# Expert rounds of a mixture-of-experts layer: the scatter of the last expert's rows ahead of the next gather

## The chip, the cores and the metric

The kernel runs on one core of one Trainium2 chip. The metric is the time of one execution on the device in microseconds (us); the figure for a kernel is the median of its runs.

## What is computed

The input is 8192 tokens of 512 float32 values. The reference is one transformer layer: layernorm, attention, layernorm and residual, then layernorm, a mixture of experts, layernorm and residual. Cut to the part that matters here:

```python
scores = softmax(xf @ gate_w.T)                 # 64 experts, 6 chosen per token
buf_tok = ...                                   # (E=64, CAP=128): rows of each expert, T where empty
gx = xp[buf_tok]                                # gather: 128 rows for each expert
g, u = split(einsum('ech,ehi->eci', gx, gate_up_proj), 2)
eo = einsum('eci,eih->ech', silu(g) * u, down_proj) * buf_w[..., None]
routed = zeros.at[buf_tok].add(eo)              # scatter with addition
shared = silu(xf @ Ws_gate) * (xf @ Ws_up) @ Ws_down
```

An expert takes at most 128 tokens. `gate_up_proj` is 512x384 for each expert and `down_proj` 192x512, all in float32.

## The kernel before, in words

Three stages follow one another. `token_pipeline` does attention, the two norms, the gate and the shared expert, 128 tokens at a time, and leaves three arrays in DRAM: `xf_d` (the normed tokens with their gate weights, 576 values a row), `acc_d` (the shared expert's output, on which the experts add) and `x1_d` (the residual). `experts` runs the 64 experts. `last_norm` reads `acc_d` back, norms it and adds the residual. The change is in `experts` alone.

In `experts` five engines run the same pipeline of iterations `j`, from -4 to 64, each with its own program order; semaphores tie them together. What belongs to expert e is spread over several iterations:

- **DVE** (the block from L1086): `gidx(j+2)` (L1088) copies the 128 row numbers of expert j+2 to one of two buffers that the gather reads. It waits for the rows of expert j, whose gather used the same buffer, and for the indices. `sidx(j-1)` (L1092) copies the row numbers of expert j-1 for the scatter, after waiting for the scatter of expert j-3 to have landed (`added`). Then `gate(j)` (L1096, which waits for the rows of j), the two halves of the gated product (L1099 and L1104, after ScalarE's tanh), the finding of the indices of expert j+3 (L1110 to L1119) and the mask `sel` for expert j+4 (L1122, L1127).
- **Pool** (from L1134) issues both indirect DMAs. The gather of expert j+2 (L1141, 128 rows of 2304 bytes) waits for `gidx(j+2)`, for `e_xT(j)` and for `gate(j)`: the last two free the one of two buffers `xg` that it fills. The scatter with addition of expert j-1 (L1148, 128 rows of 2048 bytes) waits for the output rows `eo(j-1)`, for `sidx(j-1)`, and for the scatter of j-2 to have landed, since two experts can add to the same row.
- **PE**: in iteration j, in this order: the gate and up product `gu(j)` (L1008), the transpose of the hidden rows of j-1 (L1015), the two small products that find the rows of expert j+3 (L1022, L1023), the transpose `xT(j+1)` of the gathered rows of j+1 (L1029, waits for the gather of j+1), and the down product `out(j-1)` (L1037).
- **ACT**: the copy of the transposed hidden rows of j-1 (L1050), the copy of the transposed gathered rows of j+1 (L1054), the copy `eo(j-1)` of the output from PSUM (L1058, waits for `out(j-1)` and for the scatter of j-3), tanh of j (L1062).
- **SP**: once `out(e)` is done, it loads the weights of expert e+4 into the place of e's, 768 KB and 384 KB (L133, L134), and in the rounds of the first loop, after every second expert, also 512 KB of the residual (L975). Four experts' weights are in SBUF at a time.

Pool, like the other engines, issues its instructions strictly in the order written, and a wait holds all that is behind it. In the order of the kernel before, Pool's sequence is: gather(j+2), scatter(j-1), gather(j+3), scatter(j), and so on. So the gather that follows the scatter of expert e is that of expert e+4.

Of the kernel before, what the change touches and what calls it, by code (L numbers as in the profile page):

```python
# [34 lines left out]
U32 = mybir.dt.uint32  # L35
# [65 lines left out]
def settle(eng):  # L101

    eng.nop(nofuse=True)  # L103
# [782 lines left out]
def experts(nc, cst, w1, w2, w_in, load_expert, xf_d, acc_d, rank_d, x1_d, res, res_in):  # L886


    with ExitStack() as ctx:
        def sb(name, shape, dt=F32):  # L890
            return ctx.enter_context(nc.sbuf_tensor(name, shape, dt))

        def count(name, per=1, n=1, place=0):
            return Count(ctx.enter_context(nc.semaphore(name)), per, E, n, place)
# [18 lines left out]
        idx = sb("idx", [CAP, E], I32)  # L913
        gidx = sb("gidx", [CAP, 2, 1], I32)
        sidx = sb("sidx", [CAP, 2, 1], I32)
        xg = sb("xg", [P, 2, D + E])
# [10 lines left out]
        x_got = [count(f"x_got{n}", 16, 2, n) for n in range(2)]  # L927
        added = count("added", 16)
        e_xT = count("e_xT")
# [7 lines left out]
        ed_gidx = count("ed_gidx")  # L937
        ed_sidx = count("ed_sidx")
        ed_gate = count("ed_gate")
# [15 lines left out]
        def active(e):  # L955
            return not isinstance(e, int) or 0 <= e < E

        def pipeline(eng, iteration):
            for j in range(FIRST, LOOP):
                iteration(j, j % NW)  # L960
            with eng.Fori(0, ROUNDS) as r:
                for u in range(NW):
                    iteration(r * NW + (LOOP + u), (LOOP + u) % NW)
            for j in range(REST, LAST):
                iteration(j, j % NW)
# [100 lines left out]
        @block.vector  # L1066
        def _(dve):
            dve.wait_ge(start, 32)
            nc.vector.tensor_copy(tri[:], c[0:NT, C_TRI:C_TRI + NT]).then_inc(setup, 1)
            nc.vector.tensor_copy(base[:, :, 0], c[0:NT, C_TILE:C_TILE + 1].broadcast_to([NT, E]))  # L1070
            nc.vector.memset(base[:, :, 2], 1.0)
            dve.wait_ge(setup, 2)
            nc.vector.tensor_copy(end[:], ends_ps[0:NT, 0:E]).then_inc(setup, 1)
            nc.vector.tensor_tensor(first[:], ends_ps[0:NT, 0:E], rank[:, :, P - 1], ALU.subtract).then_inc(setup, 1)
            dve.wait_ge(setup, 4)
            nc.vector.tensor_copy(base[:, :, 1], first[:]).then_inc(setup, 1)
            dve.wait_ge(setup, 5)

            def column(ap, e):
                return ap[:, e:e + 1] if isinstance(e, int) else ap[:, bass.ds(e, 1)]  # L1080

            def iteration(j, place):
                par = place % 2
                if active(j + 2):
                    dve.wait_ge(x_got[par].sem, x_got[par].at(j))
                    dve.wait_ge(ed_idx.sem, ed_idx.at(j + 2))  # L1086
                    settle(dve)
                    nc.vector.tensor_copy(gidx[:, par, :], column(idx[:], j + 2)).then_inc(ed_gidx.sem, 1)  # L1088
                if active(j - 1):
                    dve.wait_ge(added.sem, added.at(j - 3))  # L1090
                    settle(dve)
                    nc.vector.tensor_copy(sidx[:, 1 - par, :], column(idx[:], j - 1)).then_inc(ed_sidx.sem, 1)  # L1092
                if active(j):
                    dve.wait_ge(x_got[par].sem, x_got[par].at(j))
                    dve.wait_ge(ed_h.sem, ed_h.at(j - 1))
                    nc.vector.tensor_scalar(gate[:, par:par + 1], column(xg[:, par, D:D + E], j), 0.5, None,  # L1096
                                            ALU.mult).then_inc(ed_gate.sem, 1)
                    dve.wait_ge(ea_tanh.sem, ea_tanh.at(j))
                    nc.vector.scalar_tensor_tensor(tanh[:, par, :], tanh[:, par, :], 1.0, gu_ps[par][:, 0:I],  # L1099
                                                   ALU.add, ALU.mult).then_inc(ed_h.sem, 1)  # L1100
                    dve.wait_ge(ed_h.sem, ed_h.at(j, 1))
                    dve.wait_ge(ed_gate.sem, ed_gate.at(j))
                    dve.wait_ge(e_hT.sem, e_hT.at(j - 2))
                    nc.vector.scalar_tensor_tensor(hid[:, par, :], tanh[:, par, :], gate[:, par:par + 1],  # L1104
                                                   gu_ps[par][:, I:], ALU.mult, ALU.mult).then_inc(ed_h.sem, 1)
                if active(j + 3):
                    at = find_ps[1 - par]
                    dve.wait_ge(e_find.sem, e_find.at(j + 3))
                    settle(dve)
                    nc.vector.tensor_tensor(left[:], c[:, C_ROW:C_ROW + 1], at[:, P + 1:P + 2],  # L1110
                                            ALU.subtract).then_inc(ed_idx.sem, 1)
                    nc.vector.tensor_scalar(miss[:], at[:, P + 2:P + 3], -1.0, c[:, C_MISS:C_MISS + 1], ALU.add,
                                            ALU.mult).then_inc(ed_idx.sem, 1)
                    dve.wait_ge(ed_idx.sem, ed_idx.at(j + 3, 1))
                    nc.vector.tensor_scalar(ahead[:], at[:, 0:P], left[:, 0:1], None, ALU.is_le).then_inc(ed_idx.sem, 1)
                    dve.wait_ge(ed_idx.sem, ed_idx.at(j + 3, 3))
                    nc.vector.tensor_reduce(tin[:], ahead[:], AX.X, ALU.add).then_inc(ed_idx.sem, 1)
                    dve.wait_ge(ed_idx.sem, ed_idx.at(j + 3, 4))
                    nc.vector.scalar_tensor_tensor(column(idx[:], j + 3), at[:, P:P + 1], tin[:, 0:1], miss[:], ALU.add,  # L1119
                                                   ALU.add).then_inc(ed_idx.sem, 1)  # L1120
                if active(j + 4):
                    nc.vector.tensor_scalar(past[:], c[0:NT, C_IOTA:C_IOTA + CAP], column(first[:], j + 4), None,  # L1122
                                            ALU.is_ge).then_inc(ed_sel.sem, 1)
                    dve.wait_ge(ed_sel.sem, ed_sel.at(j + 4, 1))
                    dve.wait_ge(e_find.sem, e_find.at(j + 3))
                    settle(dve)
                    nc.vector.scalar_tensor_tensor(sel[:], c[0:NT, C_IOTA:C_IOTA + CAP], column(end[:], j + 4), past[:],  # L1127
                                                   ALU.is_lt, ALU.mult).then_inc(ed_sel.sem, 1)

            pipeline(dve, iteration)  # L1130

        @block.gpsimd
        def _(pool):
            def iteration(j, place):  # L1134
                par = place % 2
                if active(j + 2):
                    pool.wait_ge(ed_gidx.sem, ed_gidx.at(j + 2))
                    pool.wait_ge(e_xT.sem, e_xT.at(j))
                    pool.wait_ge(ed_gate.sem, ed_gate.at(j))
                    settle(pool)  # L1140
                    nc.gpsimd.indirect_dma_start(xg[:, par, :], None, xf_d, bass.IndirectOffsetOnAxis(  # L1141
                        gidx[:, par, :].bitcast(U32), 0)).then_inc(x_got[par].sem, 16)
                if active(j - 1):
                    pool.wait_ge(ea_out.sem, ea_out.at(j - 1))
                    pool.wait_ge(ed_sidx.sem, ed_sidx.at(j - 1))
                    pool.wait_ge(added.sem, added.at(j - 2))
                    settle(pool)
                    nc.gpsimd.indirect_dma_start(acc_d, bass.IndirectOffsetOnAxis(  # L1148
                        sidx[:, 1 - par, :].bitcast(U32), 0), eo[:, 1 - par, :], None,
                        compute_op=ALU.add).then_inc(added.sem, 16)  # L1150

            pipeline(pool, iteration)
            pool.wait_ge(added.sem, added.at(E - 1))
# [168 lines left out]
```

## Time and profile before

| what | value |
|---|---|
| median of 3 runs | 2307.55 us (2302.56 to 2309.64) |
| the profiled execution | 2310.43 us |
| its span | 2308.6 us |
| busy share of the span | PE 87%, DVE 62%, ACT 43%, Pool 22% |
| mean granted TensorE clock | 0.937 |
| expert rounds | from about 1675 to 2190 us |
| last_norm | from about 2190 us to the end |

The profile is of one execution, and its times run from the start of the span. The profiled execution took 1.8 us more than its span, and 2.9 us more than the median of the runs. Engine names in the rows: PE is TensorE's matmuls, PEld its weight loads, SPq the DMA queue of SyncE, POOL is GpSimd. L1148 is line 1148 of the kernel. In a timeline a row says when an instruction or a merged run of them starts, how long it lasts, and, in brackets, how long its engine was idle before and what ended that.

### The profile page before, as it was taken

Reading aid. Unit: us, or ns where it says so; the run is one execution under the profiler, and the core shown is the slowest. Engines: PE = TensorE matmul, PEld = TensorE weight load, DVE = VectorE, ACT = ScalarE, POOL = GpSimd, SP = SyncE. Lnnn points to the kernel's source line nnn. Section 1 sums busy time; section 2 is a strip of 40 time slices with the busy share of each in tenths; the row PEclk is TensorE's granted clock in tenths of the full one; section 3 lists DMA queues with packets and bytes.
Section 4 is the critical chain, followed back from the end, with each engine's and each line's share of the span. In section 5 each row is a group of like instructions: output and inputs, shape, how many; then the busy total and the mean of one; then the engine's idle time right before and its main releaser. Section 6 shows DMA issues by size and latency. Waiting matters only on the chain. (4 is left out here: it accounts for less than half of the span.)

```text
span 2308.6 us, 48488 instructions
## 1 busy us (share of the span) xinstructions
PE 2009.6 (87%) x14529; PEld 1605.4 (70%) x14529; DVE 1434.2 (62%) x3874; ACT 983.2 (43%) x1779; POOL 497.7 (22%) x741
## 2 busy tenths in 40 slices
PE   6999999999999999999999999998478777787600
PEld 4888888888888888888888888887344444444300
DVE  6677677677677677677767767766233333333298
ACT  4455555555555545545545545544112222222222
POOL 1111111111111111111111111111023333333288
PEclk8999999999999999999999999999789998898855
DMA  5333433433433333333343333332669899899597
GB/s 175 97 90 91 112 90 89 111 93 89 105 99 89 101 103 88 98 106 83 97 110 85 94 112 86 93 105 69 188 188 260 255 246 250 252 266 249 139 324 258
DMA packets 386471, 325.13 MB, mean 141 GB/s; under 512 B 286656, under 2 KB 286912, under 8 KB 386368
## 3 DMA queue, kind: packets, MB, share of 16 engines
q1 hardware_dynamic: 366912, 271.04, 41.4%
q0 software_dynamic: 14336, 35.66, 7.3%
q10 hardware_dynamic: 5184, 17.96, 2.1%
q8 instruction: 19, 0.31, 0.1%
q14 instruction: 20, 0.16, 0.0%
HBM read 203.43 MB, written 121.14 MB: 141 GB/s over the span
## 5 line engine op out<-in xcount | busy, mean ns | idle before, releaser
L864 POOL TENSOR_SCALAR ve<-mv 128x1 f32<-128x1 f32 x192 | 44.9, 234 | 1319.9 <-DVE mv L698 1319.9
L592 ACT COPY qT<-bank 48x512 f32<-48x512 f32 x256 | 268.8, 1050 | 63.9 <-PE bank L435 59.2
L459 PE MATMUL score_ps<-kT,qT 48*64 48x64 f32 x4096 | 264.9, 286 | 3.0 <-ACT kT L592 3.0
L459 PEld LDWEIGHTS score_ps<-kT,qT 48*64 48x64 f32 x4096 | 219.5, 147 | 48.7 <-issue 48.7
L715 DVE SCALAR_TENSOR_TENSOR th<-th,bank 128x192 f32<-128x192 f32 x128 | 45.3, 354 | 296.8 <-ACT th L628 296.8
L1099 DVE SCALAR_TENSOR_TENSOR tanh<-tanh,e_gu 128x192 f32<-128x192 f32 x64 | 22.7, 354 | 287.6 <-ACT tanh L1062 284.2
L1008 PE MATMUL e_gu<-w,xgT 128*128 128x384 f32 x512 | 189.1, 514 | 1.3 <-ACT xgT L1054 1.3
L442 PE MATMUL bank<-wgu,xfT 128*128 128x416 f32 x512 | 187.9, 367 | 2.4 <-ACT xfT L592 2.4
L443 PE MATMUL bank<-wgu,xfT 128*128 128x416 f32 x512 | 180.4, 352 | 0.0
L1008 PEld LDWEIGHTS e_gu<-w,xgT 128*128 128x128 f32 x512 | 105.9, 207 | 98.1 <-issue 50.4
L628 ACT ACTIVATE th<-bank 128x192 f32<-128x192 f32 x128 | 42.3, 330 | 287.4 <-PE bank L446 287.4
L1148 POOL DMA_INDIRECT acc_scratch<-eo,sidx x64 | 101.7, 1590 | 266.9 <-DMA acc_scratch<-eo,sidx 138.3
L592 ACT COPY kT<-bank 48x512 f32<-48x512 f32 x256 | 148.7, 581 | 4.7
L1037 PE MATMUL e_ps<-w,hidT 96*128 96x512 f32 x256 | 147.5, 706 | 0.9 <-ACT hidT L1050 0.9
L644 ACT ACTIVATE prob<-prob 128x512 f32<-128x512 f32 x128 | 78.8, 633 | 114.5 <-DVE prob L789 114.5
L446 PE MATMUL bank<-wgu,xfT 128*128 128x416 f32 x512 | 118.0, 353 | 0.0
L866 POOL TENSOR_TENSOR rstd<-ve,mhalf 128x1 f32<-128x1 f32 x192 | 108.8, 567 | 16.2 <-POOL ve L864 0.3
L442 PEld LDWEIGHTS bank<-wgu,xfT 128*128 128x128 f32 x512 | 97.2, 190 | 19.3 <-issue 10.6
L1054 ACT COPY xgT<-e_ps 128x512 f32<-128x512 f32 x64 | 37.4, 585 | 170.6 <-PE e_ps L1029 166.9
L442 PE MATMUL bank<-wlat,xT 128*128 128x512 f32 x256 | 108.8, 425 | 1.4 <-issue 1.4
L442 PE MATMUL bank<-wo,oT 128*128 128x512 f32 x256 | 106.8, 417 | 0.0
L443 PE MATMUL bank<-wlat,xT 128*128 128x512 f32 x256 | 102.6, 401 | 0.0
(179 smaller groups left out, 4772.2 us busy)
## 6 DMA issues: line engine op xcount, KB each, us to landing
w<-w_eg SPq DMA_DIRECT2D x64, 768.0 KB
w<-w_ed SPq DMA_DIRECT2D x64, 384.0 KB
xf_scratch<-xf SPq DMA_DIRECT2D x64, 288.0 KB, 2.1
xin<-x SPq DMA_DIRECT2D x64, 256.0 KB, 3.0
v_scratch<-v SPq DMA_DIRECT2D x64, 256.0 KB, 3.5
vbd<-v_scratch SPq DMA_DIRECT2D x128, 128.0 KB, 3.2
o_scratch<-o SPq DMA_DIRECT2D x256, 64.0 KB, 2.3
oin<-o_scratch SPq DMA_DIRECT2D x64, 256.0 KB, 2.6
```

What stands on the lines that cost most here:

```text
L442: nc.tensor.matmul(dst, a[:, 0], b[:, 0], start=(n == 0), stop=False)
L443: nc.tensor.matmul(dst, a[:, 0], b[:, 1], start=False, stop=False)
L446: last = nc.tensor.matmul(dst, a[:, 1], b[:, 0], start=False, stop=(n == len(lhs) - 1))
L459: last = nc.tensor.matmul(score_ps[64 * g:64 * g + 64, blk * 64:blk * 64 + 64], qT[:, t0:t0 + B4, :].rearrange("p t h -> p (t h)"), kT[:, ...
L592: nc.scalar.copy(dst, src).then_inc(done.sem, 1)
L644: nc.scalar.activation(pf, pf, ACT.Exp, scale=SCALE).then_inc(a_exp.sem, 1)
L715: nc.vector.scalar_tensor_tensor(th[:, n, :], th[:, n, :], 1.0, b[:, 0:I], ALU.add, ALU.mult).then_inc(d_h.sem, 1)
L864: nc.gpsimd.tensor_scalar(ve[n][:], mv[n][:, 1:2], EPS, None, ALU.add).then_inc(g_rstd[n].sem, 1)
L866: nc.gpsimd.tensor_tensor(rstd[n][:], ve[n][:], mhalf[:], ALU.pow).then_inc(g_rstd[n].sem, 1)
L1008: last = nc.tensor.matmul(gu_ps[par], xgT[:, par, n, :], w1[:, place, n, :], start=(n == 0), stop=(n == KD - 1))
L1037: last = nc.tensor.matmul(out_ps, hidT[:, n, :], w2[0:PI, (place - 1) % NW, n, :], start=(n == 0), stop=(n == 1))
L1148: nc.gpsimd.indirect_dma_start(acc_d, bass.IndirectOffsetOnAxis(sidx[:, 1 - par, :].bitcast(U32), 0), eo[:, 1 - par, :], None, compute_op= ...
```

## The change

In every iteration Pool issues the scatter of expert j-1 first and the gather of expert j+2 second, each with the waits that it had. DVE makes the copies of their indices in that order too: `sidx(j-1)` first, then `gidx(j+2)`. Nothing is added or removed, and no buffer or wait value is changed. The gather that follows the scatter of expert e is now that of expert e+3.

```diff
             def iteration(j, place):
                 par = place % 2
+                if active(j - 1):
+                    dve.wait_ge(added.sem, added.at(j - 3))
+                    settle(dve)
+                    nc.vector.tensor_copy(sidx[:, 1 - par, :], column(idx[:], j - 1)).then_inc(ed_sidx.sem, 1)
                 if active(j + 2):
                     dve.wait_ge(x_got[par].sem, x_got[par].at(j))
                     dve.wait_ge(ed_idx.sem, ed_idx.at(j + 2))
                     settle(dve)
                     nc.vector.tensor_copy(gidx[:, par, :], column(idx[:], j + 2)).then_inc(ed_gidx.sem, 1)
-                if active(j - 1):
-                    dve.wait_ge(added.sem, added.at(j - 3))
-                    settle(dve)
-                    nc.vector.tensor_copy(sidx[:, 1 - par, :], column(idx[:], j - 1)).then_inc(ed_sidx.sem, 1)
...
             def iteration(j, place):
                 par = place % 2
-                if active(j + 2):
-                    pool.wait_ge(ed_gidx.sem, ed_gidx.at(j + 2))
-                    pool.wait_ge(e_xT.sem, e_xT.at(j))
-                    pool.wait_ge(ed_gate.sem, ed_gate.at(j))
-                    settle(pool)
-                    nc.gpsimd.indirect_dma_start(xg[:, par, :], None, xf_d, bass.IndirectOffsetOnAxis(
-                        gidx[:, par, :].bitcast(U32), 0)).then_inc(x_got[par].sem, 16)
                 if active(j - 1):
                     pool.wait_ge(ea_out.sem, ea_out.at(j - 1))
                     pool.wait_ge(ed_sidx.sem, ed_sidx.at(j - 1))
                     pool.wait_ge(added.sem, added.at(j - 2))
                     settle(pool)
                     nc.gpsimd.indirect_dma_start(acc_d, bass.IndirectOffsetOnAxis(
                         sidx[:, 1 - par, :].bitcast(U32), 0), eo[:, 1 - par, :], None,
                         compute_op=ALU.add).then_inc(added.sem, 16)
+                if active(j + 2):
+                    pool.wait_ge(ed_gidx.sem, ed_gidx.at(j + 2))
+                    pool.wait_ge(e_xT.sem, e_xT.at(j))
+                    pool.wait_ge(ed_gate.sem, ed_gate.at(j))
+                    settle(pool)
+                    nc.gpsimd.indirect_dma_start(xg[:, par, :], None, xf_d, bass.IndirectOffsetOnAxis(
+                        gidx[:, par, :].bitcast(U32), 0)).then_inc(x_got[par].sem, 16)
```

## Rows read from the trace of the kernel before

**Rows 1.** The page, the span in 40 equal slices (tenths; PEclk: granted clock).
```profile
PE   6999999999999999999999999998478777787600
...
PEclk8999999999999999999999999999789998898855
DMA  5333433433433333333343333332669899899597
```

**Rows 2.** Windows view: the steady expert rounds in one stretch (PE, PEld, DVE, ACT, POOL busy).
```profile
1695.00:2173.00 478.00, 378.69 (x1218) 212.95 (x1217) 162.04 (x723) 108.05 (x244) 156.59 (x122) 0.90 0.90 249
```

**Rows 3.** Line view of L1148, 1695 to 2173 us: scatters; what ended Pool's idle time.
```profile
L1148 POOL DMA_INDIRECT acc_scratch<-eo,sidx x62: 1567/1588/1693, 1694.9 to 2172.9; - x62
...
  DMA acc_scratch<-eo,sidx: 134.1, 35
  ACT eo L1058: 71.2, 16
  DVE gate L1096: 42.1, 8
  DVE gidx L1088: 8.6, 2
```

**Rows 4.** Lines view, 1695 to 2173 us: PE's transposes of gathered rows.
```profile
L1029 PE MATMUL e_ps<-e_c,xg 128*128 128x128 f32 x244 | 49.5, 332 | 45.1 <-DMA xg<-xf_scratch,gidx 42.9
```

**Rows 5.** Timeline: from a late gather to the next scatter, clock at its lower level.
```profile
1890.11 0.17 PE L1023 MATMUL e_find<-base,sel 64*128 x1
1890.99 0.15 DVE L1092 COPY sidx<-idx 128x1 int32 x1 [1.08 <-DMA acc_scratch<-eo,sidx]
...
1894.21 1.13 PE L1029 MATMUL e_ps<-e_c,xg 128*128 128x128 f32 x4 [3.93 <-DMA xg<-xf_scratch,gidx]
...
1895.13 3.62 PE L1037 MATMUL e_ps<-w,hidT 96*128 96x512 f32 x4
...
1898.87 0.58 ACT L1058 COPY eo<-e_ps 128x512 f32<-128x512 f32 x1 [2.90 <-PE e_ps L1037]
...
1900.36 1.59 POOL L1148 DMA_INDIRECT acc_scratch<-eo,sidx  x1 [5.85 <-ACT eo L1058]
...
1902.76 0.17 PE L1023 MATMUL e_find<-base,sel 64*128 x1
```

**Rows 6.** Timeline of Pool: gathers (L1141) and scatters (L1148) in turn.
```profile
1884.58 0.99 POOL L1141 DMA_INDIRECT xg<-xf_scratch,gidx  x1 [1.32 <-PE e_ps L1029]
...
1908.68 1.59 POOL L1148 DMA_INDIRECT acc_scratch<-eo,sidx  x1 [3.85 <-DMA acc_scratch<-eo,sidx]
1910.57 0.99 POOL L1141 DMA_INDIRECT xg<-xf_scratch,gidx  x1 [0.30 <-PE e_ps L1029]
1914.50 1.59 POOL L1148 DMA_INDIRECT acc_scratch<-eo,sidx  x1 [2.93 <-DMA acc_scratch<-eo,sidx]
```

**Rows 7.** Line view of L1141, all 64 gathers: from issue to landing.
```profile
DMA to landing us min/median/max: 3.5/6.5/9.6
```

**Rows 8.** Timeline of SP's queue: loads issued after a down product has ended.
```profile
1899.00 0.34 SPq L133 DMA_DIRECT2D w<-w_eg  x1
1899.54 0.33 SPq L134 DMA_DIRECT2D w<-w_ed  x1
1900.19 0.36 SPq L975 DMA_DIRECT2D res<-x_scratch  x1
1905.69 0.33 SPq L133 DMA_DIRECT2D w<-w_eg  x1
```

**Rows 9.** The same for the gathers issued at 1884.58 and at 1903.84 us.
```profile
DMA to landing us min/median/max: 9.6/9.6/9.6
...
DMA to landing us min/median/max: 4.7/4.7/4.7
```

**Rows 10.** Windows view around that late gather (columns as in rows 2, then PEclk, DMA share, GB/s).
```profile
1890.00:1894.00 4.00, 0.28 (x2) 0.15 (x2) 0.31 (x2) 0.00 (x0) 2.07 (x2) 0.98 0.74 194
1894.00:1896.00 2.00, 1.79 (x6) 1.27 (x7) 0.00 (x0) 0.58 (x1) 0.51 (x1) 0.50 0.93 150
1896.00:1899.00 3.00, 3.00 (x5) 1.34 (x4) 0.00 (x0) 0.13 (x1) 0.00 (x0) 0.50 0.27 84
...
1902.00:1904.00 2.00, 1.88 (x12) 1.19 (x11) 0.73 (x4) 0.61 (x2) 0.16 (x1) 1.00 1.00 290
```

**Rows 11.** Timeline: the next round, clock at its upper level.
```profile
1903.00 0.72 PE L1029 MATMUL e_ps<-e_c,xg 128*128 128x128 f32 x4
...
1903.56 1.88 PE L1037 MATMUL e_ps<-w,hidT 96*128 96x512 f32 x4
```

## Prediction

> **What bounds the kernel now.** I began with the page's forty slices: the expert rounds are the stretch near slices 29 to 38, where PE is no longer full and the DMA engines are [rows 1]; only that stretch is touched. The windows view puts 62 scatters, thus 61 rounds, into it: from the scatter of expert 0 at 1694.9 to that of expert 61 at 2172.9 it is 478.0 us, **7.84 us a round** [rows 2, 3]. PE works 378.69 us of it, the DMA engines are 0.90 busy, so no engine alone fills it; it is a ring of waits with little slack. Pool's idle time before a scatter ends 35 times with the landing of the scatter before, 16 times with the output copy `eo`, 8 times with `gate` and 2 with `gidx`: the last two are waits of the gather that Pool has in front of the scatter [rows 3]. The transposes of the gathered rows already wait 42.9 us in the stretch for their DMA [rows 4]. So gathers come just in time or late though each is issued as early as its buffer is free. That is the row on which the case turns.
>
> **The change, part by part.** No instruction is added or removed: 64 gathers, 64 scatters and 128 small copies stay, at the same durations. Only order moves.
>
> DVE's swap. `sidx(j-1)` now stands ahead of `gidx(j+2)`, so its wait for scatter j-3 holds back `gidx`, `gate` and all behind. In the trace `sidx` waits for that scatter now and then (1.08 us in one row, [rows 5]), but then behind `gidx`. With scatters a longer round apart, as found below, scatter j-3 has landed by then. Cost zero; the cover is the length of the round. If it is gone, the same 1.08 us would fall on `gidx`, and Pool's gather behind it.
>
> Pool's swap. Before, the gather of e+4 followed the scatter of e. Now it is the gather of e+3. But the order on PE is transpose(e+3), then down product(e+1): iteration j has xT(j+1) ahead of out(j-1). And scatter(e+1) needs that product. So there is a closed chain, one turn for each expert: scatter(e) issued, gather(e+3) issued behind it, rows landed, xT(e+3), out(e+1), copy eo(e+1), scatter(e+1). Before, the same gather was issued one scatter earlier and its landing lay beside a whole round. Each turn is now the sum of all its steps:
>
> - scatter's start to gather's start on Pool: 1910.57 - 1908.68 = 1.89 us, where the gather waited for nothing else [rows 6]. All the gather's own waits, `gidx`, `e_xT(j)` and `gate(j)`, are of earlier work and are met;
> - gather issued to landed: the trace has 3.5 at least, 6.5 in the median and 9.6 at most [rows 7]. The stretch now has its DMA engines 0.90 busy; the same bytes over a round of 13 us make them 0.90 x 7.84 / 13 = 0.54 busy, so it should be under the median. It is not the floor, since SP puts weights, and every second time the residual, into the queues just after the down product, 0.2 to 1.4 us ahead of the scatter [rows 5, 8]. A gather 3.48 us behind such a scatter took 4.7 [rows 5, 9]. I take **5.0**, halfway between 3.5 and 6.5;
> - landing to transpose: the gather issued at 1884.58 landed 9.6 us later, at 1894.18, and its transpose began at 1894.21; I take 0.1, rounded up [rows 5, 6, 9];
> - transpose to down product: 1895.13 - 1894.21 = 0.92 us, and the product 3.62 us, where PE had stood idle for 3.93 us and the granted clock was 0.50, the 1.2 GHz level [rows 5, 10]. At the upper level it is 0.56 and 1.88 [rows 11];
> - down product's end to the start of `eo`: 1898.87 - 1898.75 = 0.12; `eo`'s start to the scatter's start: 1900.36 - 1898.87 = 1.49 [rows 5].
>
> Which clock? From the down product's end at 1898.75 PE is done with its other work of the round at 1902.93 (gu, hidden transpose, find), 4.2 us later [rows 5]. The gather lands 0.12 + 1.49 + 1.89 + 5.0 = 8.5 us after that end. So PE stands idle 4.3 us in every round, longer than the 3.93 us after which [rows 5] show the slow pair. I take the lower level for transpose and down product in all rounds, and the same cover says that the gate and up product costs nothing even when slow.
>
> A turn: 1.89 + 5.0 + 0.1 + 0.92 + 3.62 + 0.12 + 1.49 = **13.14 us**. The other ring, scatter to landing to next scatter, is shorter (1914.50 - 1908.68 = 5.82 where it bound, [rows 6]) and no longer decides; the waits for it go, and the one for the gathered rows takes their place on PE. Weights are loaded three rounds ahead, so they are not late. From scatter 0 to scatter 61 there are 61 turns, as gathers 3 to 63 all stand behind a scatter. Ahead of scatter 0 and after scatter 61 nothing changes, nor in the other stages. Sum: 61 x (13.14 - 7.84) = **+323 us**. The profiled execution, 2310.43, would become 2633.7; it stands 2.9 above the median of the runs, so I forecast 2307.55 + 323 = **2631 us**.
>
> Bounds of the landing, the only term without a row in its new place: at 3.5 the turn is 11.64 and the sum +232; at 6.5 it is 14.64 and +415; at the 9.6 of the slowest gather it would be 17.74 and +604, which every round would have to reach.
>
> **Rivals.**
>
> 1. The gather lands at its floor, 3.5 us, since traffic has thinned: 61 x (11.64 - 7.84) = +232, **2540 us**. For it: 84 GB/s only in one stretch right after a late gather [rows 10]. Against it: the loads of [rows 8] are issued anew each round just ahead. The Trainium skill, DMA: Bandwidth & Descriptors, section Anatomy of one DMA, fits such a transfer as about 2.0 us plus its bytes over 436 GB/s; for 128 rows of 2304 bytes that is an estimate of 2.7 us, with which a turn would be 10.8 and the time some 2490. The shortest of the 64 gathers here took 3.5, so the trace does not reach that figure. Chance 0.13.
>
> 2. The gather lands as now, 6.5 us or somewhat more, because what it meets is not the mean traffic but the burst just issued: 61 x (14.64 - 7.84) = +415, **2722 us**. For it: the median of all gathers [rows 7], many of which, as in [rows 6], stand straight behind a scatter. Chance 0.14.
>
> 3. The clock stays at its upper level, as in rounds whose gather is in time: the turn is 13.14 - (0.92 - 0.56) - (3.62 - 1.88) = 11.04, the sum +195, **2503 us**. Against it: [rows 5, 10]. Chance 0.07.
>
> 4. The other side, faster. The scatter is no longer held by the gather's waits: 42.1 + 8.6 = 50.7 us of Pool's idle time before scatters in the stretch [rows 3]. If the chain above did not bind, all of it could come back: 2307.55 - 50.7 = **2257 us**. It decides when the gather lands within 7.84 - (0.1 + 0.56 + 1.88 + 0.12 + 1.49) = 3.7 us of the scatter's issue, which is 1.8 us after its own issue; the shortest is 3.5. Chance 0.02.
>
> 5. The change does nothing that can be measured, if Pool's order did not bind at all (a gather that is late either way). Then 2307 us. Against: the gather is issued 1.89 us behind a scatter that needs the product before it, by program order. Chance 0.01.
>
> **How the numbers follow.** The forecast has 0.63. It is the likeliest case alone, not a mean. The range of 8 in 10 holds the forecast with landings from 3.2 to 6.6, at 61 us of time for each us of landing, and with them rivals 1 and 2: **2520 to 2730**. Rival 3, the far ends and 4 and 5 are left out. A measurement of this kernel can tell about 0.3% from no change; faster has 0.02, the same 0.01, slower 0.97: even the lowest turn I can build from rows, 1.89 + 3.5 + 0.1 + 0.56 + 1.88 + 0.12 + 1.49 = 9.54 us, is above 7.84.
>
> **What the changed profile would show.** If right: the stretch of expert rounds lasts some 320 us more, and the other two stages are as before. Pool's scatters wait for the copy `eo` nearly every time and hardly ever for a landing, each gather starts about 1.9 us behind its scatter, and the transposes' wait for the gathered rows grows from 42.9 us to about 61 x 4.3 = 260 us. The mean landing is near 5.0. The four matmuls of the down product take 3.6 us in almost every round, and the granted clock is well under 0.90. DMA share in the stretch falls from 0.90 to about 0.54. If the down products stay at 1.9 us, rival 3 holds; if landing is at 3.5 or 6.5, rival 1 or 2. I would be wrong at the root if PE did not wait for gathers longer than now, or if a scatter still waited for the scatter before it.

## The result and the profile after

The changed kernel takes **2647.88 us** in the median (2643.41 to 2650.97), the kernel before 2305.49 in the same comparison: a ratio of **1.148, 95% interval 1.145 to 1.151**. The forecast was 2631, the range 2520 to 2730. The profiled execution has a span of 2648.5 us, 339.9 more than before.

One stretch grew, that from the first scatter to the 62nd. First the line view of the scatters in it (now L1141); then, from its lines view, the down product, the scatters and the transposes:

```profile
L1141 POOL DMA_INDIRECT acc_scratch<-eo,sidx x62: 1575/1588/1632, 1694.3 to 2512.9; - x62
...
  ACT eo L1058: 631.7, 60
  issue: 23.1, 2
```
```profile
L1037 PE MATMUL e_ps<-w,hidT 96*128 96x512 f32 x244 | 216.0, 1039 | 0.0
L1141 POOL DMA_INDIRECT acc_scratch<-eo,sidx x62 | 98.5, 1588 | 654.8 <-ACT eo L1058 631.7 <-issue 23.1
...
L1029 PE MATMUL e_ps<-e_c,xg 128*128 128x128 f32 x244 | 66.9, 426 | 293.4 <-DMA xg<-xf_scratch,gidx 293.4
```

818.6 us for 61 rounds is **13.42 us a round**, against 7.84 [rows 3], and 61 x 5.58 = 340 is the whole difference. Pool no longer waits for the landing of a scatter, for `gate` or for `gidx`, which were 134.1, 42.1 and 8.6 us [rows 3]: 60 of 62 times it waits for the output copy. PE's wait for the gathered rows went from 42.9 us [rows 4] to 293.4. The windows view of the stretch, with columns PE, PEld, DVE, ACT and POOL busy, granted clock, DMA share and GB/s, answers to [rows 2]:

```profile
1694.00:2513.00 819.00, 484.23 (x1219) 262.06 (x1218) 163.00 (x724) 108.04 (x244) 158.18 (x123) 0.75 0.50 146
```

The DMA engines move the same data at a share of 0.50 where it was 0.90; the granted clock is 0.75 for 0.90, and PE's busy time has risen by 105 us for the same matmuls. One pair of rounds shows the whole closed chain. Timeline, Pool:

```profile
1965.56 1.59 POOL L1141 DMA_INDIRECT acc_scratch<-eo,sidx  x1 [9.50 <-ACT eo L1058]
1967.45 1.01 POOL L1149 DMA_INDIRECT xg<-xf_scratch,gidx  x1 [0.31 <-issue]
1980.10 1.59 POOL L1141 DMA_INDIRECT acc_scratch<-eo,sidx  x1 [11.63 <-ACT eo L1058]
1981.99 1.02 POOL L1149 DMA_INDIRECT xg<-xf_scratch,gidx  x1 [0.30 <-issue]
1992.49 1.59 POOL L1141 DMA_INDIRECT acc_scratch<-eo,sidx  x1 [9.48 <-ACT eo L1058]
```

PE:

```profile
1973.94 1.13 PE L1029 MATMUL e_ps<-e_c,xg 128*128 128x128 f32 x4 [5.80 <-DMA xg<-xf_scratch,gidx]
1974.86 3.62 PE L1037 MATMUL e_ps<-w,hidT 96*128 96x512 f32 x4
...
1986.34 1.13 PE L1029 MATMUL e_ps<-e_c,xg 128*128 128x128 f32 x4 [3.66 <-DMA xg<-xf_scratch,gidx]
1987.26 3.62 PE L1037 MATMUL e_ps<-w,hidT 96*128 96x512 f32 x4
```

And the line view of L1149 for the gather issued at 1967.45, then for the one at 1981.99:

```profile
DMA to landing us min/median/max: 6.4/6.4/6.4
...
DMA to landing us min/median/max: 4.3/4.3/4.3
```

The first turn is 1980.10 - 1965.56 = 14.54 us: 1.89 from scatter to gather, 6.4 to its landing, 0.09 to the transpose, 0.92 to the down product, 3.62 of it, 1.62 to the next scatter. The second is 12.39, and all of the difference but 0.05 is the landing, 4.3. What SP issued ahead of each of the two gathers differs by one load of the residual (L975, 512 KB):

```profile
1964.31 0.34 SPq L133 DMA_DIRECT2D w<-w_eg  x1
1964.88 0.33 SPq L134 DMA_DIRECT2D w<-w_ed  x1
1965.53 0.36 SPq L975 DMA_DIRECT2D res<-x_scratch  x1
1978.72 0.33 SPq L133 DMA_DIRECT2D w<-w_eg  x1
1979.26 0.33 SPq L134 DMA_DIRECT2D w<-w_ed  x1
```

Long and short turns alternate for 56 turns, 14.65 and 12.38 us in the mean. In the last five, when SP has no more of the residual to load, all are short (12.67, 11.98, 12.78, 12.16, 12.12).

The other stages stayed: `last_norm`'s windows show the same 0.50 clock, 0.83 DMA share and 285 GB/s in both kernels.

### The profile page after: what moved, and what is told of

Read it like the earlier page. It is cut to its first block and busy times, and to the rows that moved or that the text cites. A ratio compares the mean times of both kernels' runs of the same rounds, so it can differ in the third digit from the quotient of the medians.

```text
span 2648.5 us, 48488 instructions
## 1 busy us (share of the span) xinstructions
PE 2113.9 (80%) x14529; PEld 1653.9 (62%) x14529; DVE 1434.4 (54%) x3874; ACT 983.3 (37%) x1779; POOL 498.6 (19%) x741
## 5 line engine op out<-in xcount | busy, mean ns | idle before, releaser
L1029 PE MATMUL e_ps<-e_c,xg 128*128 128x128 f32 x256 | 69.5, 422 | 295.6 <-DMA xg<-xf_scratch,gidx 295.6
L1029 PEld LDWEIGHTS e_ps<-e_c,xg 128*128 128x128 f32 x256 | 45.3, 217 | 301.4 <-DMA xg<-xf_scratch,gidx 301.3
L1141 POOL DMA_INDIRECT acc_scratch<-eo,sidx x64 | 101.6, 1587 | 663.0 <-ACT eo L1058 631.7
L1037 PE MATMUL e_ps<-w,hidT 96*128 96x512 f32 x256 | 221.8, 1019 | 0.9 <-ACT hidT L1050 0.9
L1008 PE MATMUL e_gu<-w,xgT 128*128 128x384 f32 x512 | 205.2, 549 | 1.3 <-ACT xgT L1054 1.3
L1008 PEld LDWEIGHTS e_gu<-w,xgT 128*128 128x128 f32 x512 | 120.6, 236 | 127.6 <-issue 86.2
L1037 PEld LDWEIGHTS e_ps<-w,hidT 96*128 96x128 f32 x256 | 75.5, 324 | 65.7 <-issue 64.4
L442 PE MATMUL bank<-wlat,xT 128*128 128x512 f32 x256 | 108.7, 425 | 1.4 <-issue 1.4
```

Of the source, the lines that this page charges most:

```text
L442: nc.tensor.matmul(dst, a[:, 0], b[:, 0], start=(n == 0), stop=False)
L1008: last = nc.tensor.matmul(gu_ps[par], xgT[:, par, n, :], w1[:, place, n, :], start=(n == 0), stop=(n == KD - 1))
L1029: last = nc.tensor.transpose(rowsT_ps[:, n * P:(n + 1) * P], xg[:, 1 - par, 0:D].rearrange("p (i c) -> p c i", c=KD)[:, n, :], ident)
L1037: last = nc.tensor.matmul(out_ps, hidT[:, n, :], w2[0:PI, (place - 1) % NW, n, :], start=(n == 0), stop=(n == 1))
```

## The experiments

The theory: the place of the gather behind the scatter of the expert before closes a chain, whose steps simply add up. Rivals: DVE's swap has a share; a gather behind a scatter is slow in the queue; the buffers hold the gather back; the clock is not part of it.

**The two halves of the change.** First DVE's swap alone (the first two blocks of the diff), then Pool's swap alone.

> The kernel before with DVE's swap alone; Pool keeps its order. Theory (the chain through Pool's order costs the time, DVE's swap costs nothing): 2305 us, ratio 1.00, scatter to scatter 7.8 us as before. Rival (the wait for scatter j-3 ahead of gidx and gate delays the gathers): up to 1.08 us more in each round in which sidx waits, 7 to 20 of 61, so 2315 to 2330.

> The kernel before with Pool's swap alone; DVE keeps its order. Theory: all of the loss is here, 2648 us, ratio 1.148, the same 13.4 us round as in the changed kernel. Rival (half of it is DVE's order): clearly under 2600.

Measured: DVE's swap alone 2305.13 us, ratio 1.0005 (0.9991 to 1.0018). Pool's swap alone 2647.36, ratio 1.150 (1.148 to 1.152). The whole loss is Pool's order. In DVE's half the copy `sidx` waited for a scatter 11 times, and nothing came of it:

```profile
  DMA acc_scratch<-eo,sidx: 9.5, 11
```

**Half the dose.** Pool's swap in every second iteration only (`gather()` stands for the gather with its waits).

```diff
+                if par == 0:
+                    gather()
                 if active(j - 1):
...
-                if active(j + 2):
...
+                if par == 1:
+                    gather()
```

> The changed kernel with Pool's swap in every second iteration only, the old order in the others. Theory (a closed chain scatter, gather, landing, transpose, down product, copy, scatter): every second turn is the long one of some 13.4 us, the turn between has its gathered rows already and takes about 7, so a pair takes 20.4 against 2 x 7.8: 30 x 4.7 = about +145, 2450 us, range 2420 to 2500. Rival (the gather behind the scatter just lies longer in the DMA queue): the late gathers are half as many and the loss is half, 2476, but the rounds are all alike.

Measured: 2476.27 us, ratio 1.075 (1.073 to 1.077). The total is by chance also the rival's number, so the rounds have to decide, and they are not alike. Pool's timeline (L1152 scatters, L1142 gathers):

```profile
1907.72 1.59 POOL L1152 DMA_INDIRECT acc_scratch<-eo,sidx  x1 [5.04 <-ACT eo L1058]
1909.61 1.02 POOL L1142 DMA_INDIRECT xg<-xf_scratch,gidx  x1 [0.30 <-issue]
1911.88 0.98 POOL L1142 DMA_INDIRECT xg<-xf_scratch,gidx  x1 [1.25 <-DVE gate L1096]
1921.62 1.63 POOL L1152 DMA_INDIRECT acc_scratch<-eo,sidx  x1 [8.76 <-ACT eo L1058]
1928.31 1.58 POOL L1152 DMA_INDIRECT acc_scratch<-eo,sidx  x1 [5.06 <-ACT eo L1058]
1930.20 1.04 POOL L1142 DMA_INDIRECT xg<-xf_scratch,gidx  x1 [0.30 <-issue]
1931.83 0.98 POOL L1142 DMA_INDIRECT xg<-xf_scratch,gidx  x1 [0.60 <-issue]
1942.82 1.62 POOL L1152 DMA_INDIRECT acc_scratch<-eo,sidx  x1 [10.01 <-ACT eo L1058]
```

A turn with its gather in the chain takes 13.90 and 14.51 us, the one between 6.69. The short turns are as the theory has them. The 31 long ones are 14.33 in the mean, 0.9 over the 13.4 assumed: up to the last three, the gather in the chain is here always one behind a residual load, and lands in 6.1 to 7.1 us. That is 29 us more, of which the short turns (6.69 for 7) give back 9, so it makes 20 of the 26 us by which 2450 was missed.

**The clock.** Matmuls with unused results (filler) on PE ahead of its wait for the gathered rows, first four, then seven.

```diff
+                if active(j) and active(j - 1):
+                    for n in range(4):
+                        nc.tensor.matmul(ends_ps[:, 0:C_MISS], ident, c[:, 0:C_MISS], start=True, stop=True)
                 if active(j + 1):
                     pe.wait_ge(x_got[1 - par].sem, x_got[1 - par].at(j + 1))
```

> The changed kernel with four matmuls of 390 columns (0.98 us each at the upper clock, results unused) on PE between the finding products and the wait for the gathered rows; they fill 3.9 us of the 3.6 to 5.9 us that PE stands idle. Theory (the clock's lower level after the idle wait costs 0.33 + 1.64 us of each turn): down product back to 1.9 us, round 13.4 to about 11.5, 61 x 1.97 = -120, 2528 us; 2520 to 2550 as the filler may overrun a short wait by 0.3. Rival (clock is not of the chain, or low for another reason): 2648 or more.

> As the kernel with four filling matmuls on PE, but seven. The four took 2.9 us instead of 3.9 and left the clock low in about every second round, in which the wait is the longer one (2571 us). Seven take some 5.1 us at the upper clock. Theory (clock costs 0.33 + 1.64 us of each turn, after any long idle wait): all down products at 1.9 us, but in the rounds with the short wait of 3.6 us the filler overruns it by up to 1.5 us: gain 61 x 1.97 = 120, loss up to 30 x 1.5 = 45, so 2530 to 2575 us. Rival (the level has nothing to do with the idle wait): down products of 3.6 us remain and the time is over 2600.

Measured: four give 2570.69 us (ratio 1.115, 1.113 to 1.117), outside what was expected; seven give 2561.02 (1.110, 1.107 to 1.113), inside. Two rounds of the four:

```profile
1991.42 2.89 PE L1027 MATMUL e_ps<-e_c 128*128 128x390 f32 x8
1997.12 0.75 PE L1032 MATMUL e_ps<-e_c,xg 128*128 128x128 f32 x4 [2.81 <-DMA xg<-xf_scratch,gidx]
1997.70 2.48 PE L1040 MATMUL e_ps<-w,hidT 96*128 96x512 f32 x4
...
2004.32 2.89 PE L1027 MATMUL e_ps<-e_c 128*128 128x390 f32 x8
2008.15 0.75 PE L1032 MATMUL e_ps<-e_c,xg 128*128 128x128 f32 x4 [0.95 <-DMA xg<-xf_scratch,gidx]
2008.74 1.88 PE L1040 MATMUL e_ps<-w,hidT 96*128 96x512 f32 x4
```

The filler lasts 2.89 us, not the 3.9 that I had made of eight rows of 0.49: these overlap. Where 2.81 us of idle wait are left, the down product is partly slow; where 0.95 are left, it is not. Seven of them:

```profile
1927.31 4.85 PE L1027 MATMUL e_ps<-e_c 128*128 128x390 f32 x14
1932.00 0.63 PE L1032 MATMUL e_ps<-e_c,xg 128*128 128x128 f32 x4
1932.47 1.88 PE L1040 MATMUL e_ps<-w,hidT 96*128 96x512 f32 x4
...
1938.63 4.85 PE L1027 MATMUL e_ps<-e_c 128*128 128x390 f32 x14
1944.25 0.75 PE L1032 MATMUL e_ps<-e_c,xg 128*128 128x128 f32 x4 [0.77 <-DMA xg<-xf_scratch,gidx]
1944.83 1.88 PE L1040 MATMUL e_ps<-w,hidT 96*128 96x512 f32 x4
```

The median matmul of the down product goes back from 1057 to 592 ns, and the whole product takes 1.88 us in all but three of the 61 turns. The kernel is 87 us shorter, though PE does 4.85 us more work in each round. So the clock is part of the loss: 87 of 342 us are shown, a quarter. The working from the steps, 61 x (0.33 + 1.64) = 120 us, would make it a third. What is missing fits the filler, which overruns the wait in every second round (no idle ahead of 1932.00): those turns go from 12.38 to 11.23, by 1.15 and not by 1.97, and the long ones from 14.65 to 12.63. The Trainium skill, TensorE: Matmul & The Clock Gate, Part 1, has it that the slow state is the default and activity lifts it; these runs agree, 1.88 against 3.62 us for the same four matmuls, by whether PE worked or stood in the wait ahead.

**What the slow landings meet.** The residual loads out of the rounds.

```diff
-            with sp.Fori(1, 1 + WITH_X1) as r:
-                load_round(r, True)
-            with sp.Fori(1 + WITH_X1, E // NW) as r:
+            with sp.Fori(1, E // NW) as r:
                 load_round(r, False)
+            for g in range(EARLY, NT // G):
+                load_group(g)
```

> The changed kernel with the 28 residual loads of 512 KB taken out of the rounds and issued after the last weights. Theory (the gathers of odd experts land in 6.6 us and those of even ones in 4.4 because after every second down product 512 KB more stand in the queues): all gathers land in about 4.5, scatter to scatter 12.4 in every round, 61 x 1.1 = -65 us in the rounds; the 14.7 MB come behind, 52 us at 280 GB/s, of which some 40 lie beside the last four rounds: 2590 us, 2575 to 2640. Rival (odd and even gathers differ for another reason, as the buffer or the rows): they stay at 6.6 and 4.4 and the rounds at 14.5 and 12.4.

Measured: 2611.81 us, ratio 1.132 (1.129 to 1.135). Line view of the gathers, 1700 to 2360 us, in this kernel:

```profile
L1149 POOL DMA_INDIRECT xg<-xf_scratch,gidx x52: 988/999/1019, 1709.8 to 2350.2; - x52
...
DMA to landing us min/median/max: 4.2/4.6/5.7
```

In the changed kernel the same stretch has 4.2/4.7/7.2. The landings over 5.7 us are gone, and Pool's timeline has nearly equal turns, here 12.47 and 12.67:

```profile
1909.02 1.59 POOL L1141 DMA_INDIRECT acc_scratch<-eo,sidx  x1 [9.69 <-ACT eo L1058]
...
1921.49 1.59 POOL L1141 DMA_INDIRECT acc_scratch<-eo,sidx  x1 [9.57 <-ACT eo L1058]
...
1934.16 1.59 POOL L1141 DMA_INDIRECT acc_scratch<-eo,sidx  x1 [9.77 <-ACT eo L1058]
```

The expected 2590 was missed by 22 us, though the range held. The first 59 turns are 12.59 us in the mean and not 12.4, which makes 11 of them. Nor did the loads lie beside the last four rounds: SP waits for expert 59's down product first, and its queue has them, all 28 in one run, only when two turns of the chain are left. Those two take 16.75 and 15.54 us, 7 more than two others; the rest is not traced:

```profile
2437.51 31.42 SPq L975 DMA_DIRECT2D res<-x_scratch  x28
```

**Depth, order or buffers.** Four buffers for gathered rows and their indices in three kernels; to make room, `tanh` has one buffer instead of two in all three, and two masks share one. First with the order and the depth of the changed one, and waits of two experts earlier:

```diff
-                    pool.wait_ge(e_xT.sem, e_xT.at(j))
-                    pool.wait_ge(ed_gate.sem, ed_gate.at(j))
+                    pool.wait_ge(e_xT.sem, e_xT.at(j - 2))
+                    pool.wait_ge(ed_gate.sem, ed_gate.at(j - 2))
```

> The changed kernel, gather of e+3 behind the scatter of e as there, but with four buffers for gathered rows and indices, so that a gather waits for nothing of the two experts before; tanh has one buffer instead of two and two masks share one, to make room. Theory (the place in Pool's order closes the chain, buffers are not what makes it late): 2648 us, within 0.5%. Rival (the gather is late because its buffer, gate or transpose waits are late): down towards 2305.

Then the scatter first, but the gather one expert further ahead:

```diff
                 if active(j - 1):
...
-                if active(j + 2):
-                    pool.wait_ge(ed_gidx.sem, ed_gidx.at(j + 2))
-                    pool.wait_ge(e_xT.sem, e_xT.at(j))
-                    pool.wait_ge(ed_gate.sem, ed_gate.at(j))
+                if active(j + 3):
+                    slot = (place + 3) % NW
+                    pool.wait_ge(ed_gidx.sem, ed_gidx.at(j + 3))
+                    pool.wait_ge(e_xT.sem, e_xT.at(j - 1))
+                    pool.wait_ge(ed_gate.sem, ed_gate.at(j - 1))
```

> The changed kernel with the scatter still first in each iteration of Pool, four buffers as in the run beside it, and the gather one expert further ahead: iteration j issues scatter j-1, then gather j+3 (its index copy moves to the end of DVE's finding of those indices). Theory (depth decides, not which of the two comes first): the gather behind scatter e is that of e+4 again, and the loss goes: 2260 to 2310 us, below 2305 if the scatter's waits for gate and gidx (50 us in the kernel before) were worth something. Rival (a gather behind a scatter is what is slow): 2500 or more.

And the kernel before, gather first and gather j+2 as there, with the waits of the first diff:

> The kernel before, gather first, with four buffers for gathered rows and indices, so that gather j+2 waits for nothing of expert j but its indices (the same room-making as in the other kernels with four buffers). It tells whether at the old depth the order of the two on Pool matters. Theory (depth decides; at equal depth the order is worth nothing that shows): 2295 to 2310 us, as before and as the kernel with the scatter first and the gather one expert further (2300 us). Rival (the scatter in front is itself worth something at that depth, as its 50 us of waits for gate and gidx suggest): this kernel is slower than 2300 by over 0.3%, or, if freeing the gather is what helps, clearly under 2300.

Measured: 2652.21 us for the first (1.150, 1.147 to 1.153): buffers alone do nothing. 2300.21 for the second (0.9971, 0.9955 to 0.9988): **with one expert more of depth, the scatter can stand first and the loss is gone**. 2302.02 for the third (0.9991, 0.9979 to 1.0002). So with enough depth the order makes no difference that these runs can show: the intervals of the second and the third kernel overlap. In the second kernel a gather still starts right behind a scatter (L1142 scatters, L1151 gathers):

```profile
1909.68 1.59 POOL L1142 DMA_INDIRECT acc_scratch<-eo,sidx  x1 [6.26 <-DVE sidx L1087]
1911.57 1.00 POOL L1151 DMA_INDIRECT xg<-xf_scratch,gidx  x1 [0.30 <-issue]
1915.38 1.59 POOL L1142 DMA_INDIRECT acc_scratch<-eo,sidx  x1 [2.81 <-DMA acc_scratch<-eo,sidx]
1917.27 0.99 POOL L1151 DMA_INDIRECT xg<-xf_scratch,gidx  x1 [0.30 <-DVE sidx L1087]
```

The next scatter comes 5.70 us later and does not wait for that gather's landing. So the rival that a gather behind a scatter is slow in itself falls. The landings say the same: over all gathers of a kernel their median is 6.0 us here and 6.5 in the kernel before, and only 4.6 in the changed one, the slow one. What the swap changed is who waits for a landing; the landing itself did not grow.

**Do the terms add up?** Filler and late residual loads in one kernel.

> The changed kernel with both terms taken away at once: six filling matmuls on PE (some 4.2 us at the upper clock, the wait being some 4.1 with the residual loads out of the rounds) and the residual loads behind the last weights. Theory (the turn is a plain sum of its steps): 12.6 us without the residual loads, less 1.64 + 0.33 for the clock, plus 0.3 for overrun: 10.9 to 11.1 us a round up to the last four, 61 x (11.0 - 12.7) = -104 against the kernel with the residual loads last (2612): 2508 us, 2490 to 2530. Rival (the terms overlap, since a shorter turn brings the loads of one round into the next): 2530 or more.

Measured: 2509.43 us, ratio 1.090 (1.088 to 1.092), where 2508 was expected. In the first 59 turns the terms add up: 10.77 us in the mean, against 12.59 with the late residual loads alone and 7.84 before. With these two terms gone some 205 of 342 us are left. 59 x 2.93 = 173 of them are what remains of each of these turns, the bare order. 16 more are in the last two turns, 16.98 and 14.98, where the residual loads stand in the queues, the gathers land in 9.0 and 7.5 us, and PE is idle again; there the slow down product is back too:

```profile
2344.91 1.13 PE L1032 MATMUL e_ps<-e_c,xg 128*128 128x128 f32 x4 [5.71 <-DMA xg<-xf_scratch,gidx]
2345.83 3.62 PE L1040 MATMUL e_ps<-w,hidT 96*128 96x512 f32 x4
```

## Why the prediction was right

- **The chain** (Pool's swap): right, shown by the two halves, by the half dose and by the depth. Scatter to gather was forecast at 1.89 us and is 1.89; the copy and Pool's start 1.61 and 1.62.
- **DVE's swap costs nothing**: right, 1.0005.
- **The clock**: right in what it costs. 3.62 was forecast for every down product; the mean is 216.0 / 61 = 3.54. Its reason, an idle wait of over 3.93 us in each round, held for every second round and the last five. In the others PE waits 3.4 to 3.9 us, and the product takes 3.16 to 3.62 all the same. Rival 3, that the level stays up, falls: it held only in the runs that kept PE at work.
- **The landing**, 5.0 us: the one term that was mis-sized. The turn of 13.42 less all other steps, 1.89 + 0.1 + 0.9 + 3.54 + 0.12 + 1.49, leaves 5.4, and the landings of the 61 gathers read one by one have a mean of 5.42. That is +24 us, of which a shorter down product gives back 5; with the landing right, the sum would be 2631 + 24 - 5 = 2650, and 2648 was measured. What the prediction put as one value between floor and median is two kinds: 4.2 to 4.8, mean 4.4, where the loads issued just before are the weights alone, and 5.6 to 7.3, mean 6.6, where the residual's 512 KB follow them. The late residual loads take the second kind away. No gather of the stretch landed in 5.0: that a value halfway between two figures of the old trace came within 0.4 us of the mean is in part luck. Rival 2's 6.5 is right for 28 of the 61 rounds; rival 1's 3.5, with its thinner traffic, is met in none.
- **DMA share**: forecast 0.54, found 0.50; PE's wait for the gathered rows forecast 260 us, found 293.4, of which the longer landing makes some 24.
- **The other side** (rival 4): the 50.7 us of waits for `gate` and `gidx` did vanish from the list of Pool's waits before scatters, and were worth nothing beside the chain. With the depth given back the kernel with the scatter first gains 6 us in the medians (2300.21 against 2305.91; by the interval 3 to 10), and at that depth Pool still waited for `gate` and index copies. Rival 5, no change, falls with the ratio of 1.148.
- The Trainium skill's fit of a transfer (DMA: Bandwidth & Descriptors, Anatomy of one DMA) would have a gather land in an estimated 2.7 us. The shortest gather anywhere in the changed kernel took 3.3 us, and with 4.2 at least in the rounds the trace does not agree.

## What to carry to other kernels

When two operations on one in-order queue change places, ask which *instance* each now stands behind, not just which kind: here gather(e+4) behind scatter(e) became gather(e+3), and the engine that feeds the scatter needs that gather first, so a prefetch turned into a step of a closed loop. Such a loop is costed by adding its steps from single rows, with the clock level that the longer wait will bring, and the cure is the old order or one unit more of depth; buffers alone cure nothing. The Trainium skill's advice to issue a transfer early and wait for it late (DMA: Bandwidth & Descriptors, Rules for kernel authors) is what was given up, and the price here was 15%.

## What the runs showed that I had not expected

- A gather's landing depends on what was put into the queues 2 to 3 us before it: 4.4 us in the mean behind 1152 KB of weights, 6.6 with 512 KB more, while the DMA engines are only 0.50 busy over the stretch. The mean share says little about what one transfer meets.
- 14 matmul passes of 390 columns, whose rows say 491 ns each, took 4.85 us in all, 0.35 each: durations in rows overlap, and an estimate from them for a run of matmuls is a third or more too long.
- Adding 4.85 us of unused matmuls a round made this kernel 87 us faster (2561 against 2648).
